# Decoder layer on one core: three flipped key tiles for every second head of nine groups, with another order of the projections in a group

## What is computed

```python
def _L0_xattn_ref(Q, K, V, Wq, bq, Wk, bk, Wv, bv, Wo, bo):
    q = (Q @ Wq + bq).reshape(b, len_q, H, DIM_K).transpose(0, 2, 1, 3)
    k = (K @ Wk + bk).reshape(b, K.shape[1], H, DIM_K).transpose(0, 2, 1, 3)
    v = (V @ Wv + bv).reshape(b, V.shape[1], H, DIM_V).transpose(0, 2, 1, 3)
    scale = 1.0 / np.sqrt(b).astype(np.float32)
    att = jax.nn.softmax(jnp.einsum('bhqd,bhkd->bhqk', q * scale, k), axis=-1)
    out = jnp.einsum('bhqk,bhkd->bhqd', att, v)
    return out.transpose(0, 2, 1, 3).reshape(b, len_q, H * DIM_V) @ Wo + bo

x = _layernorm(x + _L0_attn_ref(x, L0_attn_W), axis=-1)
x = _layernorm(x + _L0_xattn_ref(x, ctx_1024, ctx_1024, ...), axis=-1)
x = _layernorm(x + _L0_ffn_ref(x, ...), axis=-1)
```

## Time and profile before

| | us |
|---|---|
| median of 3 runs | 1870.48 |
| lowest and highest | 1868.18, 1873.57 |
| the profiled execution | 1871.99 |
| its span, first to last instruction | 1870.0 |
| self-attention, until the first scores of the cross-attention | about 354 |
| the 16 groups | about 354 to 1643 |
| feed-forward | about 1643 to 1870 |

### The profile page before, as it was taken

The page is one execution under the profiler, slowest core; times in us unless marked ns, Lnnn a source line. Parts: engine busy times, 40 slices in busy tenths (PEclk is TensorE's granted clock), DMA queues, the critical chain, the costliest instruction groups (busy, mean ns, idle before and its releaser), DMA issues.

```text
span 1870.0 us, 28844 instructions
## 1 busy us (share of the span) xinstructions
PE 1844.4 (99%) x8863; PEld 1521.2 (81%) x8863; DVE 1573.8 (84%) x3386; ACT 1159.4 (62%) x2461; POOL 1042.6 (56%) x1108
## 2 busy tenths in 40 slices
PE   9999999989999999999999999999999999999998
PEld 8888888768888888888888888888888877778887
DVE  6676666789898998989899898998989899968887
ACT  5544554467677676776777777776777777632221
POOL 2322233246667676656656566566656666756773
PEclk9999999999999999999999999999999999999999
DMA  6777787976859786585776858576585866622121
GB/s 225 276 291 278 283 301 274 317 263 189 259 161 312 215 265 221 156 266 152 252 252 193 265 164 270 180 234 219 168 259 173 252 212 184 194 96 91 60 77 68
DMA packets 200920, 400.39 MB, mean 214 GB/s; under 512 B 18112, under 2 KB 82112, under 8 KB 198592
## 3 DMA queue, kind: packets, MB, share of 16 engines
q1 hardware_dynamic: 164720, 329.08, 54.2%
q10 hardware_dynamic: 36048, 69.48, 11.2%
HBM read 211.31 MB, written 88.08 MB: 160 GB/s over the span
## 4 chain that ended last, share of the span: by engine, by line
PE 90%; DVE 5%; DMA 2%; ACT 1%; POOL 1%; issue 1%; ACTq 0%; POOLq 0%; DVEq 0%
PE a_proj L1429 17%; PE a_turned L1429 17%; PE a_av L1468 11%; PE a_score L1442 11%; PE a_proj L48 9%; PE a_proj L1852 5%; PE a_av L1852 5%; PE a_score L48 3%; PE a_av L48 3%; PE a_turned L1452 3%; PE a_proj L1452 3%; DVE all_negmax L1242 1%; DMA all_second_buffer<-x1T_scratch 1%; DVE c_squares L1298 1%; PE a_score L1827 1%; PE a_turned L624 1%
## 5 line engine op out<-in xcount | busy, mean ns | idle before, releaser
L1021 POOL TENSOR_SCALAR c_prob<-c_prob,all_rden 128x512 f32<-128x512 f32 x512 | 352.1, 695 | 496.3 <-DVE all_rden L1248 496.2
L1106 ACT ACTIVATE c_prob<-a_score,all_negmax 128x512 f32<-128x512 f32 x512 | 347.5, 684 | 195.6 <-DVE all_negmax L1242 192.5
L1242 DVE TENSOR_REDUCE all_negmax<-a_score 128x1 f32<-128x512 f32 x512 | 328.8, 684 | 92.3 <-PE a_score L1442 92.2
L1028 POOL TENSOR_TENSOR c_landing<-c_landing,c_flip_hi 128x512 fp32r<-128x512 f32 x250 | 318.4, 1295 | 2.1 <-ACT c_flip_hi L1156 2.0
L1298 DVE STREAM_TRANSPOSE c_squares<-c_prob 128x256 f32<-128x256 f32 x500 | 291.3, 621 | 1.0 <-POOL c_prob L1021 1.0
L1442 PE MATMUL a_score<-c_ks,c_qs 128*128 128x512 f32 x1024 | 277.1, 392 | 9.7 <-ACT c_prob L1106 9.0
L1442 PEld LDWEIGHTS a_score<-c_ks,c_qs 128*128 128x128 f32 x1024 | 190.1, 188 | 56.5 <-issue 8.4
L1468 PE MATMUL a_av<-c_pt,c_vs 128*128 128x512 f32 x512 | 158.3, 391 | 0.0
L343 POOL TENSOR_SCALAR s_prob<-s_prob,s_rden 128x512 f32<-128x512 f32 x32 | 22.2, 694 | 227.5 <-DVE s_rden L515 227.5
L1156 ACT CAST c_flip_hi<-c_landing 128x512 fp32r<-128x512 f32 x250 | 143.3, 625 | 1.4 <-issue 1.3
L1429 PE MATMUL a_proj<-all_third_buffer,all_first_buffer 128*128 128x512 f32 x552 | 138.2, 399 | 0.6 <-DVE c_ks L1267 0.6
(11 more groups left out here) (230 smaller groups left out, 4028.5 us busy)
## 6 DMA issues: line engine op xcount, KB each, us to landing
c_landing<-c_squares SPq DMA_DIRECT2D x500, 128.0 KB, 2.7
c_wk<-wk_scratch SPq DMA_DIRECT2D x64, 512.0 KB, 3.9
c_wq<-wq_scratch SPq DMA_DIRECT2D x64, 512.0 KB, 4.5
c_ks<-c_ks SPq DMA_DIRECT2D x128, 256.0 KB, 3.7
all_first_buffer<-ctxT_scratch ACTq DMA_DIRECT2D x60, 512.0 KB, 8.5
all_second_buffer<-x1T_scratch ACTq DMA_DIRECT2D x60, 512.0 KB, 7.2
ctxT_scratch<-s_csp SPq DMA_DIRECT2D x8, 2048.0 KB, 7.4
c_y<-y_steps_scratch SPq DMA_DIRECT2D x16, 1024.0 KB, 5.6
```

What stands on the lines that cost most here:

```text
L1021: nc.gpsimd.tensor_scalar(prob[:, n % 2, i, :], prob[:, n % 2, i, :], rden[:, n % 2, i:i + 1], 1.0, ALU.mult, ALU.mult).then_inc(p_ready, 1)
L1028: nc.gpsimd.tensor_tensor(whole, as_f32(whole), by_square(as_f32(flip_hi_part[:, k, :])), ALU.subtract).then_inc(flip_lo, 1)
L1106: nc.scalar.activation(prob[:, n % 2, i, :], spsum[:, i % 2, :], ACT.Exp, bias=negmax[:, n % 2, i:i + 1], scale=1.0, accum_out=den[:, n % ...
L1242: nc.vector.tensor_reduce(negmax[:, n % 2, i:i + 1], spsum[:, i % 2, :], AX.X, ALU.max, negate=True).then_inc(smax, 1)
```

## The change

1. A list `THIRD` names heads n = 1, 3, 5, 7 of groups 4 to 12, 36 heads. For these, three key tiles are flipped (k = 1, 2, 3) and one is turned (k = 0). `turned_in` is empty in their odd step.
2. Their block transposes are 128x384 and their DMAs 192 KB, with buffers of their own (`third_squares`, `third_landing`, `third_hi`). The high part of the third tile is copied by ACT at the start of step 2n+2 (`third_head`), and POOL makes its low part at the start of the same step, before its scaling; `values` uses it in step 2n+3.
3. The tables of projections are in another order: in a middle group, V2 stands in step 1 of its own group instead of in step 15 of the group before, and the others stand about one step later. The first group has one item fewer, the last one more.
4. The buffer `x2` is allocated by each stage, the new buffers lie where it was, and two waits keep the uses apart.

```diff
-    NEXT = ["V0+", "K0+", "Q0+", "V1+", "K1+", "V2+"]
-    MIDDLE = ["Q1", "K2", "Q2", "V3", "O0", "O1", "K3", "Q3", "O2", "O3"] + NEXT
-    FIRST = ["V2", "K2", "", "V3", "", "Q2", "K3", "", "Q3", "", "V0+", "K0+", "V1+", "Q0+", "K1+", "V2+"]
-    LAST = ["Q1", "", "V3", "K2", "Q2", "K3", "O0", "Q3", "", "O1", "", "O2", "", "O3", "", ""]
-    HALVED = {0: (5, 8), GROUPS - 1: (2, 9, 11, 13)}
+    NEXT = ["K0+", "V0+", "Q0+", "K1+", "V1+"]
+    MIDDLE = ["Q1", "V2", "K2", "V3", "Q2", "O0", "K3", "Q3", "O1", "O2", "O3"] + NEXT
+    FIRST = ["V2", "K2", "", "V3", "", "Q2", "K3", "", "Q3", "", ""] + NEXT
+    LAST = ["Q1", "V2", "K2", "V3", "Q2", "K3", "O0", "Q3", "", "O1", "", "O2", "", "O3", "", ""]
+    HALVED = {0: (5, 8), GROUPS - 1: (9, 11, 13)}
...
+    THIRD = [h for g in range(4, GROUPS - 3) for h in range(HH * g + 1, HH * g + HH, 2)]
+
+    def flipped_of(head):
+
+        return T - TURNED + (head in THIRD)
...
     def turned_in(g, step):
 
         n, half = divmod(step, 2)
+        if HH * g + n in THIRD and half:
+            return []
...
+    def third_head(g, step):
+
+        n = step // 2 - 1
+        return None if step % 2 or HH * g + n not in THIRD else (g, n) if n >= 0 else (g - 1, HH - 1)
...
             if landed_head(g, step):
-                for k in range(FLIPPED):
+                for k in range(TURNED, T):
                     flip_lo_tile(*landed_head(g, step), k)
+            if third_head(g, step):
+                flip_lo_tile(*third_head(g, step), TURNED - 1)
             for tile in ahead(g, step):
                 norm_tile(*tile)
...
             if landed_head(g, step) and not (last and step == STEPS - 1):
-                for k in range(FLIPPED):
+                for k in range(TURNED, T):
                     flip_hi_tile(*landed_head(g, step), k)
+            if third_head(g, step):
+                flip_hi_tile(*third_head(g, step), TURNED - 1)
             if item and item[0] != "O":
                 proj_hi_part(item)
...
-            if letter == "V" and j == 0:
+            if letter in "KV" and j == 0:
                 pe.wait_ge(c_loaded[k], 16 * G + 16)
```

56 lines of the change are left out of this document (39 added, 17 removed).

## The result

| | before | after |
|---|---|---|
| median of the runs, us | 1872.03 (1868.18 to 1874.07, 4 runs) | 1856.53 (1855.08 to 1857.46, 4 runs) |
| ratio | | 0.9915, 95% interval 0.9901 to 0.9929 |
| profiled execution, its span, us | 1871.99, 1870.0 | 1857.34, 1855.3 |

The change makes the kernel 15.5 us faster by the medians and 14.7 us by the spans of the two profiled executions. 1860.0 was predicted, with a range of 1852.5 to 1870. So the total is right, but it is a sum of errors that partly cancel, which is luck as much as reading.

A forecast was written before the change was run, and what follows sets the result against it. PE's instructions were taken to bound middle groups. Turns -12.8, context and x -1.8, group 0 -2.9, last group +0.7, waits +3.5, +1.8, +0.9, +0.3 sum to -10.3 from 1870.5: 1860.2, given as 1860.0 us, range 1852.5 to 1870.

The forecast's parts named there:

- turns: PE, odd steps of groups 4 to 12: 36 turns removed at 0.355 us each, -12.8 us.
- context and x: Loads needed one step later by the new order, so PE's waits in groups 6 and 14 go: -1.8 us.
- last group: The item that leaves group 0 reappears in the last group's first three steps: +0.7 us.
- group 0: V0 of group 1 leaves step 10, so the next scores start at about 410.0 instead of 412.92: -2.9 us.
- Wait 1: ACT's copy of head 3's third tile, before step 8's exponentials, waits for DMAs landing past 13.3 us: +3.5 us.
- Wait 2: POOL in steps 2 to 4: scalings and low parts late for PE, 0.2 us a group, +1.8 us.
- Wait 3: DVE: Q0's low part, one step ahead of its scores, late by 0.1 us, +0.9; steps 14 and 15, +0.3.
- other groups' V and K in new places: Moved projections elsewhere fall on DVE's lighter steps and cost nothing.
- A: Rival: landings in time, POOL and DVE never late, all waits zero; 1853.7 us; chance 0.2.
- B: Rival: DVE becomes the bound, a threefold transpose costing 0.6 us more rather than 0.27; 1873 us; chance 0.08.
- C: Rival: head 3's landing holds ACT in every group, 20 us instead of 3.5; 1876.5 us; chance 0.12.
- D: Rival: group 0's time is only given back by the last group, 3 us less gain; 1863; within forecast's 0.55.

The follow-up runs named there:

- Experiment 1: Kernel after with `THIRD` empty: new order of projections, every head flipped as before; 1870.96 us, ratio to before 0.9993.
- experiment 8: Kernel after with one more 512 KB transfer in front of head 3's four DMAs in groups 4 to 12; 1865.71 us, ratio to before 0.9969.
- experiment 2: Kernel after with the projection tables of before, `THIRD` kept (flips without the new order); 1878.7 us, ratio to before 1.0040.
- experiment 7: Kernel after with one more wide DVE transpose in each of the 36 heads, read by nothing; 1866.75 us, ratio to before 0.9971.
- experiment 6: Kernel after with the store of y started in step 12 instead of 10, WO as it was; 1858.89 us, ratio to before 0.9937.
- experiment 9: Kernel after with WO loaded in steps 1 and 2 of the next group, group 0's empty slot filled; 1850.92 us, ratio to before 0.9883.
- experiment 10: Kernel after with WO loaded one piece a step in steps 0 to 3, group 0's empty slot filled; 1850.32 us, ratio to before 0.9891.
- experiment 3: Kernel after with WO's loads in steps 13 and 14 instead of 10 and 11; 1854.66 us, ratio to before 0.9908.

## Why the prediction was right, and where it was not

**The sum.** A span of 1859.7 us was predicted and 1855.3 measured. Term by term it missed by -4.5 us (turns), -6.5 (waits), -1.1 (context and x) and -0.3 (last group), and by +2.5 (group 0), +4.9 (group 8) and +0.6 ahead of the cross-attention. That the total came within 4.4 us is partly luck. The groups themselves came out at 78.3 us, below the 79 to 81 that were to show the forecast.

**What bounds the kernel:** right. PE is never idle in a typical middle group, before or after, and PE work that goes away shows in full.

**Turns, predicted -12.8, measured -17.3.** The term was too small by a third. The distance from a turn's start to the next matmul, 0.355 us, is not its whole price; the twelve matmuls behind it take 0.13 us more than without it, most of it at the first. The rows for this were there: a step of the kernel before without a turn doesn't exist in the middle groups, but 18 matmuls at the distance of 0.227 us that the section on the profile gives are 4.09 us, and the odd step took 4.57. Experiment 1 against the kernel after gives 0.48 us for each of 36 turns.

**Waits 1 to 3, predicted +6.5, measured 0.** Their mechanisms exist, their thresholds were not passed. Wait 1: the form was right and the threshold nearly (13.7, not 13.3, experiment 8). What failed was the step that took group 6's landing of 13.6 us in one execution as a property of the group and added 1.3 to 1.9 to it; in the kernel after it came at 12.2 there, and in experiment 1, with the squares of before, at 11.3 there and at 13.5 in group 7. Wait 2: experiment 2 shows it, with 4.8 us in 16 waits, when K2 stands in step 1; in the kernel after V2 stands there, and a margin of about 0.17 us is left (experiment 7), where the prediction had it 0.16 late. That is thin: single groups of experiments 6, 9 and 10 pay 0.2 to 0.5 us for it. Wait 3: a wide flip costs 0.23 us more, close to the 0.27 that was taken, and Q0's low part ends 4.26 us after step 13's scores, as its chain of 4.2 to 4.3 says. The deadline of 4.35 was too early (in experiment 7 the scores start 0.06 us after the low part ends), and 0.1 us was counted though the chain was in time; about 0.26 us are left. The Trainium skill ("Vector Engine (DVE) Microarchitecture Reference", the section on the reshape front-end) gives the transpose one element per cycle per lane; the 231 ns for 128 elements more, 1.8 ns an element, don't agree with it. But this transpose reads every fourth element of a row, and no run has one that reads them in order, so whether the transpose or its reading makes the difference is not shown.

**Context and x, predicted -1.8, measured -2.9.** Groups 6, 7 and 14; the term missed group 7 and what follows group 14's wait. Experiment 2 shows what the order is for: without it PE waits 16.1 us for context and x, in 18 places.

**Group 0, predicted -2.9, measured -0.4, and -3.0 in experiment 1.** The scores did move forward as said, but in the profiled execution the low clock behind a wait of 3.25 us took 2.6 us back. The prediction didn't think of the clock.

**The last group, predicted +0.7, measured +0.4.** Right in kind.

**What wasn't in the sum: group 8, +4.9 against 78.33.** The order puts O3, and with it the store of y, a step later, right in front of the load of K1's weights, in the one middle group that also loads WO. The prediction read the waits of middle groups and took "other groups' V and K in new places" at nothing. It named DVE as their cover, and did not follow the store of 1 MB to the 512 KB of weights behind it. Experiment 1 has the delay without the flips, and experiments 3 and 6 show that the crowding of WO and the store makes most of it.

**The rivals.** A (1853.7, all margins hold) was nearest in mechanism: its waits were all zero. With turns at their true price it would have been 1849; the missing 7 us are group 8 (4.9) and the low clock in group 0 (2.5). B fell: DVE is not the bound, though 0.26 us from it at one step. C fell for the kernel after, but experiment 8 shows its mechanism with a threshold of 13.7 us. D was half right: the time of group 0 was not given back by the last group, but by the clock.

## What to carry to other kernels

Read the price of an instruction that you remove from the step with it and a step without it, not from the distance to its neighbour. When a change makes the bounding engine faster, list every load that it will ask for earlier, and look first at the rare groups that load something more. When you move an item, follow the stores and loads that wait for it to what they will stand in front of. Where transfers fill the queues, 2 MB of weights have no place that is free by themselves: cut them into pieces, put one in each step, and end before their first use by at least one crowded landing.

## What the runs showed of the hardware that was not expected

- The granted clock was either 1.00 or 0.50 in the cross-attention. It fell to 0.50 in or just behind idle stretches of PE of 1.76, 1.90, 2.35, 2.38, 3.08 (three times), 3.25 and 3.26 us, and at one of 1.88 that 0.92 more followed a microsecond later. It stayed at 1.00 behind 1.74, 2.97, 3.17 and 3.19 us, behind 3.25 in group 8 of experiment 7, and behind all up to 1.58. So the length of the wait alone does not tell. Behind waits of 2.97 to 3.26 us at one and the same place it fell in three executions of six. A fall cost 1.6 to 2.6 us.
- A turn of four 128x128 transposes delays what follows the twelve 128x512 matmuls behind it by 0.13 us; the second of the twelve starts 0.316 us after the first instead of 0.227, the others 0.227 to 0.234 apart.
- A load of 512 KB has a median of 4.1 us for `wk`, 7.8 for the context, and took 12.3 us beside WO, the store of y and the squares, with 334 GB/s in all.
